# Half-width products for the odd class of the correlation scores, and the weight transpose issued before the row store

## The reference, cut to what matters

```python
def _autocorrelation(Q, K, V):            # H = 8 heads, d = 256, L = 512
    qf = jnp.fft.fft(q, axis=2)
    kf = jnp.fft.fft(k, axis=2)
    corr = jnp.fft.ifft(qf * jnp.conj(kf), axis=2).real
    topk = int(C * np.log(L))             # 12
    w, idx = jax.lax.top_k(corr.transpose(0, 1, 3, 2), topk)
    w = jax.nn.softmax(w, axis=-1)
    pos = jnp.arange(L)[:, None]
    for i in range(topk):
        g = jnp.minimum(idx[:, :, None, :, i] + pos, L - 1)
        out = out + w[:, :, None, :, i] * jnp.take_along_axis(v, g, axis=2)

x = x + _autocorrelation(_layernorm(x), ctx, ctx)         # x, ctx: (8, 512, 2048)
x = x + ffn(_layernorm(x))      # x W^T + bias + a sum of 16 low-rank products
```

## Time and profile before

| | |
|---|---|
| time, median of 3 runs | 2644.93 us (2644.93 to 2651.17) |
| profiled execution, its own time | 2646.18 us |
| its span | 2644.4 us (1.8 us less) |
| granted PE clock, mean | 0.984 |
| PE, DVE, ACT, POOL busy | 2497.7, 1901.7, 1055.7, 2155.5 us |

### The profile page before, as it was taken

The page is one execution under the profiler, slowest core; times in us unless marked ns, Lnnn a source line. Parts: engine busy times, 40 slices in busy tenths (PEclk is TensorE's granted clock), DMA queues, the critical chain, the costliest instruction groups (busy, mean ns, idle before and its releaser), DMA issues.

```text
span 2644.4 us, 36606 instructions
## 1 busy us (share of the span) xinstructions
PE 2497.7 (94%) x12288; PEld 1559.9 (59%) x12288; DVE 1901.7 (72%) x4966; ACT 1055.7 (40%) x1906; POOL 2155.5 (82%) x1558
## 2 busy tenths in 40 slices
PE   4999866799999999999999999999999999999998
PEld 3655555566666656666666666666666666654444
DVE  5989989778787788777877788778876688645000
ACT  4788855533443343533443334533333233201000
POOL 5799999778998799988998899888998899654222
PEclk8999978899999999999999999999999999999999
DMA  9399998966788687966887687957786687758853
GB/s 325 99 261 269 269 244 198 231 192 209 254 266 228 219 252 238 277 203 210 258 270 210 217 275 248 271 181 236 253 250 172 219 265 243 199 203 301 268 180 114
DMA packets 550028, 613.19 MB, mean 232 GB/s; under 512 B 322640, under 2 KB 448720, under 8 KB 532176
## 3 DMA queue, kind: packets, MB, share of 16 engines
q1 hardware_dynamic: 549840, 610.86, 76.6%
HBM read 383.22 MB, written 151.00 MB: 202 GB/s over the span
## 4 chain that ended last, share of the span: by engine, by line
PE 53%; POOL 22%; DVE 8%; DMA 7%; SPq 5%; issue 4%; ACT 1%; POOLq 0%; DVEq 0%; ACTq 0%
PE f_ps L840 11%; PE f_ps L844 11%; PE f_ps L842 11%; PE a_ps L718 7%; PE a_ps L805 5%; PE a_ps L763 4%; POOL a_zu L1115 4%; POOL f_x1p L1115 4%; POOL a_rows L1115 3%; DMA a_w_lag<-a_w_row 2%; PE a_ps L821 2%; PE a_ps L820 2%; POOL a_zv L1115 2%; POOL a_zf L1115 2%; PE a_ps L768 1%
## 5 line engine op out<-in xcount | busy, mean ns | idle before, releaser
L840 PE MATMUL f_ps<-f_whi,f_hhi 128*128 128x512 f16 x2048 | 777.3, 380 | 5.6 <-issue 2.4
L844 PE MATMUL f_ps<-f_whi,f_hlo 128*128 128x512 f16 x2048 | 777.4, 380 | 0.0
L842 PE MATMUL f_ps<-f_wlo,f_hhi 128*128 128x512 f16 x2048 | 777.4, 380 | 0.0
L924 ACT ACTIVATE a_side<-a_ps 128x256 f32<-128x256 f32 (+1 forms) x320 | 128.0, 416 | 873.5 <-PE a_ps L805 698.4
L844 PEld LDWEIGHTS f_ps<-f_whi,f_hlo 128*128 128x128 f16 x2048 | 200.6, 98 | 242.3 <-issue 1.1
L842 PEld LDWEIGHTS f_ps<-f_wlo,f_hhi 128*128 128x128 f16 x2048 | 200.7, 98 | 230.8 <-issue 1.1
L840 PEld LDWEIGHTS f_ps<-f_whi,f_hhi 128*128 128x128 f16 x2048 | 200.7, 98 | 220.6 <-issue 6.7
L1115 POOL TENSOR_TENSOR a_prod<-a_prod,a_tf 128x512 f32<-128x512 f32 x128 | 160.2, 1273 | 138.7 <-DVE a_tf L1242 138.7
L1115 POOL TENSOR_TENSOR a_zv<-a_zv,a_tw 128x512 f32<-128x512 f32 x128 | 183.3, 1450 | 100.5 <-DVE a_tf L1242 100.5
L805 PE MATMUL a_ps<-inv,a_prod 128*128 128x256 f32 x1024 | 239.5, 388 | 25.6 <-POOL a_prod L1115 25.6
L1115 POOL TENSOR_TENSOR f_x1p<-f_x1p,f_y 128x512 f32<-128x512 f32 x128 | 172.7, 1381 | 101.0 <-DVE f_y L1242 101.0
(11 more groups left out here) (137 smaller groups left out, 5236.6 us busy)
## 6 DMA issues: line engine op xcount, KB each, us to landing
f_whi<-whi_scratch SPq DMA_DIRECT2D x128, 512.0 KB, 5.1
f_wlo<-wlo_scratch SPq DMA_DIRECT2D x128, 512.0 KB, 6.5
a_rows<-in_x_dram SPq DMA_DIRECT2D x62, 1024.0 KB, 8.7
vs<-in_ctx_dram SPq DMA_DIRECT2D x64, 512.0 KB, 6.2
xs<-in_x_dram SPq DMA_DIRECT2D x64, 512.0 KB, 8.0
parts_scratch<-a_so SPq DMA_DIRECT2D x64, 512.0 KB, 7.5
x_scratch<-a_rows SPq DMA_DIRECT2D x32, 1024.0 KB, 5.1
f_x1p<-x_scratch SPq DMA_DIRECT2D x32, 1024.0 KB, 6.8
```

The costliest lines, as they stand in the source:

```text
L840: nc.tensor.matmul(f_ps[:, t, :], h_hi[q][:, kq, rows_t], w_hi[u % WR][:, :, kq, :], start=(k == 0), stop=False)
L842: nc.tensor.matmul(f_ps[:, t, :], h_hi[q][:, kq, rows_t], w_lo[u % WR][:, :, kq, :], start=False, stop=False)
L844: mm = nc.tensor.matmul(f_ps[:, t, :], h_lo[q][:, kq, rows_t], w_hi[u % WR][:, :, kq, :], start=False, stop=(k == DB - 1))
L924: return nc.scalar.activation(out, source, ACT.Copy, **how)
```

## The change

In `correlate` the two full-width products of the odd class (256 columns each, summed in PSUM) become two products of 128 columns each, not summed: the sine product for the lags [128, 1..127], the cosine product for the lags [0, 255..129]. For the odd class the sine is the same at lag n and 256-n and the cosine changes its sign, so the two half products hold everything: DVE, after ACT's copy, forms sine minus cosine and sine plus cosine for the 127 paired lags (two new instructions per group), and only then does its two old ones, behind a wait on a new semaphore. The weights loaded into PE are as many as before. In SP's list `turn_weights` moves ahead of `store_x1` and `load_attn`.

```diff
@@ sync
                 if at and at[1] == 7:
                     for q in range(2):
                         load_h(at[0] + 1, q)
+                if turned_by_dma(w):
+                    turn_weights(w)
                 if r is not None:
                     store_x1(w, r)
                     if r % TB < TB - 1:
@@
-                if turned_by_dma(w):
-                    turn_weights(w)
                 if at:
                     load_weights(unit + 3)
@@ tensor, correlate
                 for g in range(SUB):
-                    for cls in range(2):
-                        for k in range(2):
-                            mm = nc.tensor.matmul(corr[:, g, cls * 2 * T:(cls + 1) * 2 * T],
-                                                  prod[:, 2 * k + cls, g * T:(g + 1) * T],
-                                                  inv[:, cls, k, :], start=(k == 0), stop=(k == 1))
+                    for k in range(2):
+                        nc.tensor.matmul(corr[:, g, 0:2 * T], prod[:, 2 * k, g * T:(g + 1) * T], inv[:, 0, k, :],
+                                         start=(k == 0), stop=(k == 1))
+                    nc.tensor.matmul(corr[:, g, 2 * T:3 * T], prod[:, 3, g * T:(g + 1) * T], inv[:, 1, 1, 0:T],
+                                     start=True, stop=True)
+                    mm = nc.tensor.matmul(corr[:, g, 3 * T:4 * T], prod[:, 1, g * T:(g + 1) * T],
+                                          inv[:, 1, 0, T:2 * T], start=True, stop=True)
                     mm.then_inc(corr_mm, 1)
@@ vector, part_corr
                     dve.wait_ge(odd_moved, SUB * n + g + 1)
+                    by_sine, by_cosine = corr[:, g, 2 * T + 1:3 * T], side[:, g, T + 1:2 * T]
+                    nc.vector.tensor_tensor(side[:, g, 1:T], by_sine, by_cosine, ALU.subtract)
+                    nc.vector.tensor_tensor(by_cosine, by_sine, by_cosine, ALU.add).then_inc(odd_whole, 1)
+                    dve.wait_ge(odd_whole, SUB * n + g + 1)
                     even, odd = corr[:, g, 0:2 * T], corr[:, g, 2 * T:4 * T]
                     nc.vector.tensor_tensor(odd, even, side[:, g, :], ALU.subtract)
                     nc.vector.tensor_tensor(even, even, side[:, g, :], ALU.add).then_inc(corr_folded, 1)
```

More of the change, by code:

```diff
@@ L338, in flow @@
         odd_moved = sem("a_odd_moved")
+        odd_whole = sem("a_odd_whole")
         corr_parted = sem("a_corr_parted")
```

## The result

The changed kernel is slower: 2685.01 us (2682.57 to 2688.84, four runs) against 2644.93, a ratio of 1.0149 with a 95% interval of 1.0127 to 1.0171. Forecast were 2597 us, 0.982. The profiled execution took 2687.18 us (span 2685.4), 41.0 more than the one of before.

A forecast was written before the change was run, and what follows sets the result against it. PE was taken to bound windows 21 to 28, POOL and DVE to pace windows 1 to 8. From 2646.2 us, - 42.5 - 23.8 + 4.4 + 14 = -47.9 gave 2598.3, as median 2597; range 2589 to 2607, with rivals 2581 to 2616.

The forecast's parts named there:

- PE, the halved products: `correlate`: eight half-width records at 0.110 us instead of 0.216 save 0.85 us a chunk, 42.5 us in total.
- Rival 1: `correlate`: half the columns cost nearly the whole price, saving only 0.17 us a chunk; 2620 us, chance 0.10.
- The spacing rule of the Trainium skill: PE's load and matmul pairs: about 81 ns apart at 128 columns, 131 at 512, so only 0.14 us saved a chunk.
- SP, the transposes first: SP's queue in row windows: transposes no longer wait for POOL's rows; all 23.8 us of stalls go, delayed store costs nothing.
- DVE, the four new instructions: DVE's folds: 0.55 us a group, hidden in PE-bound windows; 4.4 us lost in windows 1 to 13, bounds 0 and 14.
- the pause of 0.76 before `a_so`: DVE in windows 1 to 8: its next idle time absorbs 0.76 of the 1.1 us delay, leaving 0.3 us a window.
- What takes the place of the stall: POOL: Row windows: PE waits for late POOL at `output` and `queries`, 2.5 us a batch, 14 us in all, bounds 0 to 41.
- Rival 4: DVE late to `part_corr` in every window, 1.1 us added to each of 64; slower, 2692 us, chance 0.03.

## Why the prediction was wrong, point by point

- **PE, the halved products: right.** 0.11 us a record, 0.84 us a chunk against 0.85; 41.2 us of the 41.7 forecast for windows 14 to 62 (the 0.8 for window 63 is not to be seen: 327.8 us behind its start, before 327.7). Rival 1 is refuted by the 0.22 us for two records. The spacing rule of the Trainium skill (TensorE: Matmul & The Clock Gate, Back-to-back issue gap) does not hold for these pairs either.
- **SP, the transposes first: right about PE's wait, wrong about what the wait was for others.** The 23.8 us of stalls for the transposes went, although in window 26 the first of them still took 5.2 us to land and not under 4, and the delayed store cost nothing. But I called the stall pure loss. It was also the time in which POOL caught up before `row_low`.
- **DVE, the four new instructions: 4.4 us forecast, some 9.4 measured** (of the 10.6 before window 14, 1.2 come before window 1). The cost of the instructions was right, 0.51 us a group against 0.55. The failed step is that the pause of 0.76 before `a_so` would take up the delay. It doesn't: in window 5 the maxima, ScalarE's exponents, its copy `a_vk`, PE's `output` (8.4 us behind DVE's first fold instruction before, 9.5 now) and the copy for `a_so` all come 1.0 us later, and the pause with them. For windows 9 to 13 the forecast of 2.0 us was too high: they lost nothing.
- **What takes the place of the stall: POOL. 14 us forecast.** PE's waits for a late POOL were about 5.4 us (0.8 in windows 18, 26, 34, 42, 50, and 1.3 in window 60). The step failed in what it left out: I followed POOL's lateness only into PE's `output` and `queries`, and took DVE's instructions for independent of POOL. `row_low` shut out is 5 x 15.84 + 10.5 = 89.7 us, the waits with what the lower clock adds behind them. The sum with the measured terms is - 41.2 - 23.8 + 10.6 + 5.4 + 89.7 = 40.7.
- **Rival 4** had the right side and the wrong mechanism: it wanted DVE to be late by its own work in all windows, and windows 21 to 24 are at 35.46; that its 2692 us lie near the measured 2685 is chance. No rival had an instruction whose length depends on another engine. The trace of before already showed the contention: `row_low` lasted from 2.28 to 5.59 us.

## What to carry to other kernels

Before a stall is removed, list who else uses it: here it spaced POOL's work so that a VectorE subtraction on two SBUF tiles found its turn. An instruction whose duration varies in a profile (2.3 to 5.6 us here) is no constant in a sum; find what it shares with another engine and what happens if that engine never pauses. Narrow GpSimd instructions inside an unbroken chain are suspect: a change of the place of one by two instructions was worth 75 us, and a change of the tiles' addresses goes with any added tile.

## What the runs showed of the hardware that was not expected

A VectorE subtraction of 2.28 us on two SBUF tiles was shut out for up to 22.6 us behind back-to-back GpSimd adds. In isolation one add of 256 columns on 1 to 96 partitions did it in every later phase of the unbroken chain, adds over 128 partitions never; two such adds cancelled, a pause ended it. In the kernels it also happened behind 128x512 adds, with no narrow add in the chain, and ended eleven times during a one-row add; why is open. Where it got its turn at the end of the add in progress, the GpSimd add behind it took 3.3 us instead of 1.26.
